# Turning summed tiles back by DMA transposes instead of by TensorE, in a long convolution followed by a quantised feed-forward layer

## The chip, the cores and the metric

One core of a Trainium2 chip runs the whole program. The metric is the time of one execution on the device in microseconds (us), the median of several runs. The engines are TensorE (PE, with its weight loads PEld), VectorE (DVE), ScalarE (ACT), GpSimd (POOL) and SyncE (SP, which here only issues DMAs).

## The reference, cut to what matters

The input `x` is (8, 512, 1024), the context (8, 512, 1024), and there are 64 heads of 8 channels. The first layer (the mixer) takes products of context channels, convolves them over the sequence, and sums them with the normalised input:

```python
kv = einsum('bhil,bhjl->bijhl', k_, v_)              # k = v = context: 8 x 8 products for each head
y = irfft(rfft(kv, 2L) * rfft(ssm_kernel, 2L))[..., :L]   # a causal convolution over L = 1024
out = y + kv * D
out = einsum('bijhl,bhil->bjhl', out, q_)            # q = layernorm(x): summed over i
x = x + tanh(g_xattn) * out                          # the residual
x = x + tanh(g_ffn) * ffn(layernorm(x))              # ffn: layernorm, two linear layers with
                                                     # inputs and weights quantised by blocks of 32
```

The change lies wholly in the way in which `out` gets back to the rows of `x` and is added to them.

## The kernel before, in words

The program has two parts, one after the other: `mixer_block` and `ffn_block`. The change touches the first.

**Heads and tiles.** The mixer goes through 64 heads (`h`), two to a tile (`t = h // 2`, 32 tiles, `TILE_HEADS` = 2). A tile is 128 rows of `x` (2 heads x 8 channels x 8 batches) by 1024 positions. In what follows an even head is the first of its tile, an odd head the second.

**One head.** Positions lie on the partitions while a head is convolved. ACT copies the context tile to PSUM (`copy_k`, L385) and squares it (`squares`, L392); DVE multiplies the other pairs (`make_kk`, L529, L532). ACT rounds the products to their high half (`high_half`, L399), DVE takes the rest (`low_half`, L538). PE multiplies 26 blocks of the convolution three times each, 78 matmuls in five stretches (`conv_stretch`, L328), into a single PSUM tile `y_ps`. DVE multiplies `y_ps` by `q` in two parts (`times_q`, L552, L555, L558) into the two `terms` tiles, and POOL folds each part in four adds (`sum_part`, L763, L765, L767, L769) into `mixed[t % 2]`. PE may start head h + 1 only when `low_half(h + 1)` is done and DVE has read part 0 of head h; a product part may be written only when POOL has folded the one before it in the same `terms` tile.

**Normalising x for q.** For each tile ACT takes the mean and the spread (`ln_stats`, L436, L438, L441), POOL the inverse root (L752), ACT applies both (`ln_apply`, L445, L451). The 32-bit values are then turned by DMA: ACT splits them into low and high 16-bit halves (`split_halves`, L407, into the space of `taps`), SP issues one DMA transpose of both halves (`turn_halves`, L239, into the space of `taps_hi`), and ACT joins them into `q_ext` (`take_q`, L417).

**Turning back.** In an odd head PE transposes the finished tile of the previous pair, `mixed`, by eight matmuls against the identity (`turn_back`, L359) into PSUM (`turn_ps`), after the first stretch of that head. DVE adds `x_tile` to it (`residual`, L681) ahead of `times_q(h, 0)`, and SP stores the sum. PSUM's `turn_ps` is also used four times to spread weight scales (`spread_inverses`, L345), which ACT copies out (`keep_inverses`).

**Other work in the heads.** Each engine's order is written out in a loop over `h`; nothing schedules it but the position in that loop and the semaphores. Weight maxima (L638) come in 32 pieces, up to head 33; then the scales of the weights (L663 to L671) in head 34; then the second layer's weights are quantised in heads 35 to 63 in three steps for each of 16 tiles (`layer2_ints` L647, `layer2_clip` L652, `layer2_quant` L657). Four row tiles are normalised and quantised early, one in every four heads up to head 20 (`early_...`, L580 to L633, L473), and turned by SP's DMA transposes (`turn_early`, L232).

## Time and profile before

| | us |
|---|---|
| median of 3 runs | 1971.43 |
| lowest and highest | 1970.66, 1972.78 |
| the profiled execution, its own time | 1971.53 |
| its span in the trace | 1969.8 |
| PE busy in the span | 1875.5 (95%) |
| DVE busy | 1654.8 (84%) |
| ACT busy | 949.6 (48%) |
| POOL busy | 872.0 (44%) |

The mixer takes roughly the first 1015 us of the span. POOL and ACT have their work mostly there: the shares over the whole span say little of how full they are in it. The position of a head is found in the trace by PE's matmuls: 78 of line L328 are one head, and the first matmul of head 1 starts at 36.68 us, of head 8 at 141.63, of head 21 at 348.54, of head 35 at 560.71, of head 44 at 703.77, of head 63 at 990.11. These five stretches are called stages 1 to 5 below.

### The profile page before, as it was taken

The numbers are of one execution on the slowest core, as the hardware profiler recorded it, in microseconds if no ns is written. First come the engines' busy times: TensorE is split into PE (matmuls) and PEld (weight loads), VectorE is DVE, ScalarE is ACT, GpSimd is POOL, SyncE is SP. The second block draws the span as 40 slices with busy tenths as digits, with TensorE's granted clock in tenths as the row PEclk, the third lists the DMA queues.
The fourth block names the chain that finished last, engine by engine and source line by source line (L and its number), as shares of the span: only waits on it lengthen the run. The fifth ranks groups of instructions, "written<-read, shape, count | busy, mean of one in ns | idle before, by whom it ended". The sixth has DMA issues, their size and how long they took to land. (4 is left out here: it accounts for less than half of the span.)

```text
span 1969.8 us, 28534 instructions
## 1 busy us (share of the span) xinstructions
PE 1875.5 (95%) x11384; PEld 1474.7 (75%) x11432; DVE 1654.8 (84%) x1919; ACT 949.6 (48%) x1227; POOL 872.0 (44%) x645
## 2 busy tenths in 40 slices
PE   6999999999999999999966997999999999999998
PEld 5988888898888888898854665666777766666773
DVE  5889988999888888898789798899888888898843
ACT  5555556555555655555503542444455444444440
POOL 3888788787889889999930000000000000000000
PEclk9999999999999999999978998999999999999999
DMA  6665556677665665767558312221222121221112
GB/s 236 217 208 169 179 163 202 218 274 245 221 209 174 215 208 175 237 189 220 166 202 312 123 39 75 76 75 54 65 76 76 65 68 51 75 76 44 54 43 75
DMA packets 163749, 287.95 MB, mean 146 GB/s; under 512 B 105952, under 2 KB 105952, under 8 KB 155424
## 3 DMA queue, kind: packets, MB, share of 16 engines
q1 hardware_dynamic: 163616, 286.12, 44.2%
q8 instruction: 90, 1.47, 0.3%
q14 instruction: 43, 0.35, 0.1%
HBM read 218.91 MB, written 42.53 MB: 133 GB/s over the span
## 5 line engine op out<-in xcount | busy, mean ns | idle before, releaser
L328 PE MATMUL y_ps<-kk_hi,slab 128*128 128x352 f32 (+6 forms) x3328 | 892.7, 352 | 28.9 <-DMA slab<-taps_scratch 18.1
L328 PEld LDWEIGHTS y_ps<-kk_hi,slab 128*128 128x128 f32 x3328 | 596.7, 190 | 98.1 <-issue 29.8
L328 PE MATMUL y_ps<-kk_lo,slab 128*128 128x512 f32 (+6 forms) x1664 | 582.3, 350 | 0.0
L985 PE MATMUL acc_ps<-w_T,arena 128*128 128x512 bf16 x2000 | 439.5, 379 | 2.5
L970 PE MATMUL l_ps<-f_xq_T,w_T 128*128 128x256 bf16 x3584 | 398.3, 274 | 15.4 <-ACT arena L1031 10.7
L970 PEld LDWEIGHTS l_ps<-f_xq_T,w_T 128*128 128x128 bf16 x3584 | 352.6, 98 | 61.9 <-ACT arena L1031 11.2
L985 PEld LDWEIGHTS acc_ps<-w_T,arena 128*128 128x128 bf16 x2048 | 200.4, 98 | 238.5
L328 PEld LDWEIGHTS y_ps<-kk_lo,slab 128*128 128x128 f32 x1664 | 315.8, 190 | 34.6
L765 POOL TENSOR_TENSOR terms<-terms 128x768 f32<-128x768 f32 x127 | 334.5, 2634 | 10.0
L1031 ACT ACTIVATE arena<-l_ps,f_b 128x256 bf16<-128x256 f32 x512 | 213.4, 474 | 252.3 <-PE l_ps L970 247.4
L1280 POOL TENSOR_TENSOR f_rstd<-f_var_eps,f_neg_half 128x1 f32<-128x1 f32 x28 | 15.4, 549 | 697.7 <-DVE f_var_eps L1090 697.7
L552 DVE TENSOR_TENSOR terms<-y_ps,q_ext 128x768 f32<-128x768 f32 (+1 forms) x128 | 155.9, 1218 | 109.4 <-PE y_ps L328 109.3
L538 DVE TENSOR_TENSOR kk_lo<-kk,kk_hi 128x2304 fp32r<-128x2304 f32 x64 | 183.1, 2861 | 23.6 <-ACT kk_hi L399 23.3
L763 POOL TENSOR_TENSOR terms<-terms 128x72 f32<-128x72 f32 x127 | 144.2, 1135 | 112.6 <-DVE terms L558 112.4
L767 POOL TENSOR_TENSOR terms<-terms 128x384 f32<-128x384 f32 x127 | 181.2, 1427 | 10.0
L417 ACT COPY q_ext<-taps_hi 128x1024 int16<-128x1024 int16 x124 | 105.6, 924 | 107.3 <-DMA taps_hi<-taps 107.3
L399 ACT CAST kk_hi<-kk 128x2304 fp32r<-128x2304 f32 x64 | 136.2, 2128 | 8.2 <-DVE kk L532 6.2
L1010 ACT ACTIVATE f_n<-arena,f_shift,f_rstd 128x1024 bf16<-128x1024 f32 x28 | 34.5, 1239 | 214.2 <-POOL f_shift L1282 214.2
L385 ACT COPY k_ps<-k_ext 128x512 f32<-128x512 f32 x64 | 37.8, 590 | 199.8 <-DVE kk L532 197.0
L1038 ACT ACTIVATE arena<-arena 128x2048 bf16<-128x2048 bf16 x64 | 122.0, 1911 | 0.5
L558 DVE TENSOR_TENSOR terms<-y_ps,q_ext 128x576 f32<-128x576 f32 (+1 forms) x128 | 120.9, 945 | 0.0
L529 DVE TENSOR_TENSOR kk<-k_ps,k_ext 128x1536 f32<-128x1536 f32 x64 | 111.6, 1743 | 0.6 <-ACT k_ps L385 0.6
(130 smaller groups left out, 1880.8 us busy)
## 6 DMA issues: line engine op xcount, KB each, us to landing
slab<-taps_scratch SPq DMA_DIRECT2D x128, 512.0 KB, 4.9
arena<-in_w_m SPq DMA_DIRECT2D x32, 1024.0 KB, 6.2
arena<-x_scratch SPq DMA_DIRECT2D x60, 512.0 KB, 3.8
k_ext<-in_ctx_e SPq DMA_DIRECT2D x64, 384.0 KB, 3.4
arena<-in_w SPq DMA_DIRECT2D x18, 1024.0 KB, 6.5
x_tile<-in_x_t SPq DMA_DIRECT2D x32, 512.0 KB, 4.9
out_t<-arena SPq DMA_DIRECT2D x32, 512.0 KB, 2.6
x_scratch<-x SPq DMA_DIRECT2D x31, 512.0 KB, 3.3
```

The lines of the kernel that those rows point to most:

```text
L328: mm = nc.tensor.matmul(y_ps[:, y_base + begin:y_base + end], slab[s][:, half, d * P:(d + 1) * P], kk_part[s][:, begin - d * PAIR:end - d ...
L399: nc.scalar.copy(kk_hi[h % 2][:], kk[:].rearrange("p n c -> p (n c)")).then_inc(hi_ready, 1)
L538: nc.vector.tensor_tensor(kk_lo[h % 2][:], kk[:].rearrange("p n c -> p (n c)"), kk_hi[h % 2][:].bitcast(F32), ALU.subtract).then_inc(lo_re ...
L552: nc.vector.tensor_tensor(view(term, 0, [(pitch, count), (CH, DIAG), (1, CH)]), view(y_ps, y_at, [(PAIR, count), (CH, DIAG), (1, CH)]), vi ...
L558: nc.vector.tensor_tensor(view(term, UPPER_ROWS * CH + B, [(pitch, count), (CH + B, 3), (1, CH)]), view(y_ps, y_at + CH, [(PAIR, count), ( ...
L763: add(term[:, :, 0:FOLD], term[:, :, 0:FOLD], term[:, :, 8 * CH:8 * CH + FOLD], ALU.add).then_inc(wrapped, 1)
L765: add(term[:, :, 0:4 * CH], term[:, :, 0:4 * CH], term[:, :, 4 * CH:8 * CH], ALU.add).then_inc(four_rows, 1)
L767: add(term[:, :, 0:2 * CH], term[:, :, 0:2 * CH], term[:, :, 2 * CH:4 * CH], ALU.add).then_inc(two_rows, 1)
L970: mm = nc.tensor.matmul(l1_ps[bank % L1_BANKS][:, a, :], w1_T[:, b, k, a * P:(a + 1) * P], inputs[:, k, :], start=(k == 0), stop=(k == L / ...
L985: mm = nc.tensor.matmul(acc_ps[s][:, c * 512:(c + 1) * 512], hidden[g % 2][:, k, s * P:(s + 1) * P], w2_T[:, k, c * 512:(c + 1) * 512], st ...
L1031: done = nc.scalar.activation(hidden[g % 2][:, c, :], l1_ps[bank % L1_BANKS][:, a, :], ACT.Identity, bias=b1_c[:, c:c + 1])
L1038: nc.scalar.activation(h, h, ACT.Gelu_apprx_tanh).then_inc(gelu_ready, 1)
```

## The change

The tiles 0 to 30 are no longer turned back by PE. In an odd head ACT splits the summed tile of the previous pair into 16-bit halves (`split_mixed`) and issues a DMA transpose of them itself; in the next even head it joins the turned halves into the 32-bit tile `x1` (`merge_back`), and DVE adds `x_tile` to it in place (`residual`), now at the end of the even head's order, after `low_half`. Only the last tile still goes through PE (`turn_last`, `last_residual`). The space of the halves is shared with the turning of q, so each user waits for the other. The transposes for q and the early tiles are also issued by ACT now, not by SP. ACT's order in a head is recast: squares first, then in even heads the statistics of the next tile, then the high half, then the copy of the context. Early steps, weight maxima and what follows them start one head later; the second layer's weights are spread over 28 heads instead of 29.

```diff
-    maxima_heads = list(range(6)) + list(range(7, early_heads + 5, 2))
+    maxima_heads = list(range(6)) + list(range(8, early_heads + 6, 2))
...
-                if h % TILE_HEADS == 1 and t + 1 < tiles:
-                    turn_halves(t + 1)
-                if h % TILE_HEADS == 1 and t >= 1:
-                    store_x1(t - 1)
-                    if t + 3 < tiles:
-                        load_x(t + 3)
-                if h >= 9 and h % 4 == 1 and (h - 9) // 4 < EARLY:
-                    turn_early((h - 9) // 4)
+                if h % TILE_HEADS == 0 and t >= 2:
+                    store_x1(t - 2)
+                    if t + 2 < tiles:
+                        load_x(t + 2)
...
-                pe.wait_ge(x1_ready, spread_heads[r] // TILE_HEADS - 1)
+                if r == 0:
+                    pe.wait_ge(q_ready, 1)
+                else:
+                    pe.wait_ge(inv_kept, r)
                 for n in range(LB):
                     mm = nc.tensor.matmul(turn_ps[:, n, :], inv_rows[:, n * P:(n + 1) * P], ident_bf[:], start=True, stop=True)
                 mm.then_inc(inv_spread, 1)
 
-            def turn_back(t):
-                pe.wait_ge(sums_ready, min(2 * TILE_HEADS * (t + 1), 2 * heads - 1))
-                if t == tiles - 1:
-                    pe.wait_ge(last_sums, 1)
-                if TILE_HEADS * (t + 1) in spread_heads:
-                    pe.wait_ge(inv_kept, spread_heads.index(TILE_HEADS * (t + 1)) + 1)
-                if t == 0:
-                    pe.wait_ge(q_ready, 1)
-                else:
-                    pe.wait_ge(x1_ready, t)
+            def turn_last():
+                t = tiles - 1
+                pe.wait_ge(sums_ready, 2 * heads - 1)
+                pe.wait_ge(last_sums, 1)
+                pe.wait_ge(inv_kept, len(spread_heads))
...
-                    if h % TILE_HEADS == 1 and i == 0 and t >= 1:
-                        turn_back(t - 1)
-            turn_back(tiles - 1)
+            turn_last()
...
+                if t >= 3:
+                    act.wait_ge(mixed_turned, 16 * (t - 2))
                 nc.scalar.copy(xn_halves, xn[:].bitcast(I16).rearrange("p (l h) -> p h l", h=2)).then_inc(halves_ready, 1)
+                act.wait_ge(halves_ready, t)
+                if t >= 3:
+                    act.wait_ge(back_merged, t - 2)
+                act.dma_start(q_halves, xn_halves.rearrange("p h l -> p (h l)"), transpose=True).then_inc(halves_turned, 16)
+
+            def turn_early(u):
+                act.wait_ge(x_quant, u + 1)
+                act.dma_start(first_inputs(arena, u // GROUP)[:, :, u % GROUP * P:(u % GROUP + 1) * P], n_bf[u % 2],
+                              transpose=True).then_inc(e_turned[u % 2], 16)
+
+            def split_mixed(t):
+                act.wait_ge(sums_ready, 2 * TILE_HEADS * (t + 1))
+                act.wait_ge(halves_turned, 16 * min(t + 2, tiles - 1))
+                nc.scalar.copy(xn_halves, mixed[t % 2][:].rearrange("p n c -> p (n c)").bitcast(I16)
+                               .rearrange("p (l h) -> p h l", h=2)).then_inc(mixed_split, 1)
+                act.wait_ge(mixed_split, t + 1)
+                act.wait_ge(q_ready, min(t + 3, tiles))
+                act.dma_start(q_halves, xn_halves.rearrange("p h l -> p (h l)"), transpose=True).then_inc(mixed_turned, 16)
+
+            def merge_back(t):
+                act.wait_ge(mixed_turned, 16 * (t + 1))
+                if t >= 2:
+                    act.wait_ge(x1_stored[t % 2], 16 * (t // 2))
+                if t % 2 == 0 and 1 <= t // 2 <= EARLY:
+                    act.wait_ge(e_norm, t // 2)
+                words = view(x1[t % 2].bitcast(I16), 0, [(2, L // QB), (2 * L // QB, QB), (1, 2)])
+                source = view(taps_hi_all.bitcast(I16), 0, [(QB, L // QB), (1, QB), (LB * P, 2)])
+                nc.scalar.copy(words, source).then_inc(back_merged, 1)
...
-            ln_stats(1)
             for h in range(heads):
                 t = h // TILE_HEADS
+                if h + 1 < heads:
+                    squares(h + 1)
+                if h % TILE_HEADS == 0 and t + 1 < tiles:
+                    ln_stats(t + 1)
+                if h + 1 < heads:
+                    high_half(h + 1)
                 if h + 2 < heads:
                     copy_k(h + 2)
-                if h + 1 < heads:
-                    squares(h + 1)
-                    high_half(h + 1)
                 if t + 1 < tiles:
                     if h % TILE_HEADS == 0:
+                        if t >= 2:
+                            merge_back(t - 2)
                         ln_apply(t + 1)
                         split_halves(t + 1)
                     else:
                         take_q(t + 1)
-                        if t + 2 < tiles:
-                            ln_stats(t + 2)
-                if h >= 4 and h % 4 == 0 and h // 4 - 1 < EARLY:
+                        if t >= 1:
+                            split_mixed(t - 1)
+                elif h % TILE_HEADS == 0:
+                    merge_back(t - 2)
+                else:
+                    split_mixed(t - 1)
+                if h >= 5 and h % 4 == 1 and h // 4 - 1 < EARLY:
                     early_norm(h // 4 - 1)
+                if h >= 10 and h % 4 == 2 and (h - 10) // 4 < EARLY:
+                    turn_early((h - 10) // 4)
                 if h + 1 in spread_heads:
                     repeat_inverses(spread_heads.index(h + 1))
                 if h in spread_heads:
                     keep_inverses(spread_heads.index(h))
+            merge_back(tiles - 2)
...
-                dve.wait_ge(back_ready, t + 1)
-                if 2 <= t < tiles - 1:
-                    dve.wait_ge(x1_stored[t % 2], 16 * (t // 2))
-                if t % 2 == 0 and 1 <= t // 2 <= EARLY:
-                    dve.wait_ge(e_norm, t // 2)
-                out = x1_last if t == tiles - 1 else x1[t % 2][:]
-                nc.vector.tensor_tensor(out.rearrange("p (i k) -> p i k", i=QB),
+                dve.wait_ge(back_merged, t + 1)
+                nc.vector.tensor_tensor(x1[t % 2][:], x1[t % 2][:], x_tile[:, t % X_SLOTS, :], ALU.add).then_inc(x1_ready, 1)
+
+            def last_residual():
+                t = tiles - 1
+                dve.wait_ge(back_ready, 1)
...
-                if h % TILE_HEADS == 1 and t >= 1:
-                    residual(t - 1)
                 times_q(h, 0)
                 if h + 1 < heads:
                     low_half(h + 1)
-                if h >= 3 and h % 4 == 3 and h // 4 < EARLY:
-                    early_statistics(h // 4)
+                if h % TILE_HEADS == 0 and t >= 2:
+                    residual(t - 2)
+                if h >= 4 and h % 4 == 0 and h // 4 - 1 < EARLY:
+                    early_statistics(h // 4 - 1)
...
             times_q(heads - 1, 1)
+            residual(tiles - 2)
             last_part()
             first_ints(dve)
-            residual(tiles - 1)
+            last_residual()
...
+                if t >= 2 and part == 0:
+                    pool.wait_ge(mixed_split, t - 1)
```

ACT in an even head (head 22) before, from the copy of the context for two heads ahead to the split of the normalised tile (`k_ps` and `kk` are the context and its products, `xn` the normalised tile, `taps` the space of its halves):

```order
L385 COPY k_ps<-k_ext 128x512 [waits kk_ready,k_loaded0]
L392 ACTIVATE kk<-k_ext 128x8x64 [waits hi_ready,lo_ready,k_loaded1]
L399 CAST kk_hi<-kk 128x2304 [waits y_ready,kk_ready,squares_ready]
L445 ACTIVATE shift<-neg_mean,rstd 128x1 [waits rstd_ready]
L451 ACTIVATE xn<-x_tile,shift,rstd 128x1024 [waits halves_ready,shift_ready]
L407 COPY taps<-xn 128x2048 [waits halves_turned,xn_ready]
```

Head 22 of the changed kernel:

```order
L375 ACTIVATE kk<-k_ext 128x8x64 [waits hi_ready,lo_ready,k_loaded1]
L449 ACTIVATE xn,neg_mean<-x_tile 128x1024 [waits halves_ready,x_loaded0]
L451 ACTIVATE xn,spread_sum<-x_tile,neg_mean 128x1024 [waits mean_ready]
L454 ACTIVATE var_eps<-spread_sum 128x1 [waits spread_ready]
L382 CAST kk_hi<-kk 128x2304 [waits y_ready,kk_ready,squares_ready]
L368 COPY k_ps<-k_ext 128x512 [waits kk_ready,k_loaded0]
L420 COPY x_1<-taps_hi 128x32x32x2 [waits x1_stored1,mixed_turned]
L458 ACTIVATE shift<-neg_mean,rstd 128x1 [waits rstd_ready]
L464 ACTIVATE xn<-x_tile,shift,rstd 128x1024 [waits halves_ready,shift_ready]
L392 COPY taps<-xn 128x2048 [waits mixed_turned,halves_turned,xn_ready]
L396 DMA_TRANSPOSE taps_hi<-taps 128x16x128 [waits back_merged,halves_ready]
```

The statistics came in from the odd head and stand ahead of the high half, the join (L420) and the transpose (L396) are new on ACT.

ACT in the odd head of the same pair (head 23) before, after its high half:

```order
L417 COPY q_ext<-taps_hi 128x8x128 [waits products_ready,halves_turned]
L417 COPY q_ext<-taps_hi 128x8x64
L417 COPY q_ext<-taps_hi 128x8x128
L417 COPY q_ext<-taps_hi 128x8x64
L436 ACTIVATE xn,neg_mean<-x_tile 128x1024 [waits halves_ready,x_loaded1]
L438 ACTIVATE xn,spread_sum<-x_tile,neg_mean 128x1024 [waits mean_ready]
L441 ACTIVATE var_eps<-spread_sum 128x1 [waits spread_ready]
```

And in the changed kernel, from the squares to the second transpose:

```order
L375 ACTIVATE kk<-k_ext 128x8x64 [waits hi_ready,lo_ready,k_loaded0]
L382 CAST kk_hi<-kk 128x2304 [waits y_ready,kk_ready,squares_ready]
L368 COPY k_ps<-k_ext 128x512 [waits kk_ready,k_loaded1]
L430 COPY q_ext<-taps_hi 128x8x128 [waits products_ready,halves_turned]
L430 COPY q_ext<-taps_hi 128x8x64
L430 COPY q_ext<-taps_hi 128x8x128
L430 COPY q_ext<-taps_hi 128x8x64
L406 COPY taps<-mixed 128x2048 [waits halves_turned,sums_ready]
L410 DMA_TRANSPOSE taps_hi<-taps 128x16x128 [waits q_ready,mixed_split]
```

The statistics have left the odd head; the split of the summed tile (L406) and its transpose (L410) have come in, and the squares of the next even head stand behind them.

DVE in an odd head before, from the products to the low half (`x_0` is the tile `x1[0]`):

```order
L529 TENSOR_TENSOR kk<-k_ps,k_ext 128x8x192 [waits k_copied,lo_ready]
L532 TENSOR_TENSOR kk<-k_ps,k_ext 128x8x32
L681 TENSOR_TENSOR x_0<-turn_ps,x_tile 128x1024 [waits x1_stored0,back_ready]
L552 TENSOR_TENSOR terms<-y_ps,q_ext 128x3x256 [waits sums_ready,y_ready]
L555 TENSOR_TENSOR terms<-y_ps,q_ext 128x3x64
L558 TENSOR_TENSOR terms<-y_ps,q_ext 128x3x3x64
L538 TENSOR_TENSOR kk_lo<-kk,kk_hi 128x2304 [waits hi_ready,squares_ready]
```

DVE in an even head of the changed kernel, from the second products to the first of the next head:

```order
L556 TENSOR_TENSOR kk<-k_ps,k_ext 128x8x32
L576 TENSOR_TENSOR terms<-y_ps,q_ext 128x3x256 [waits sums_ready,q_ready,y_ready]
L579 TENSOR_TENSOR terms<-y_ps,q_ext 128x3x64
L582 TENSOR_TENSOR terms<-y_ps,q_ext 128x3x3x64
L562 TENSOR_TENSOR kk_lo<-kk,kk_hi 128x2304 [waits hi_ready,squares_ready]
L700 TENSOR_TENSOR x_1<-x_1,x_tile 128x1024 [waits back_merged]
```

The residual (now L700) left its place between the products and `times_q`, stands behind the low half, and reads two SBUF tiles instead of one in PSUM and one in SBUF.

## Rows read from the trace of the kernel before

**Rows 1.** The page's busy times: time, share of the span, instructions.

```profile
PE 1875.5 (95%) x11384; PEld 1474.7 (75%) x11432; DVE 1654.8 (84%) x1919; ACT 949.6 (48%) x1227; POOL 872.0 (44%) x645
```

**Rows 2.** Busy time by engine: stages 1 to 5 (length, PE, PEld, DVE, ACT, POOL; clock, DMA).

```profile
36.68:141.63 104.95, 104.95 (x572) 93.76 (x573) 90.61 (x90) 58.04 (x62) 87.04 (x62) 1.00 0.64 205
141.63:348.54 206.91, 200.34 (x1065) 178.79 (x1063) 186.58 (x187) 116.91 (x124) 167.78 (x121) 0.98 0.57 182
348.54:560.71 212.17, 211.04 (x1155) 188.48 (x1154) 188.99 (x161) 119.40 (x127) 171.86 (x120) 1.00 0.70 242
560.71:703.77 143.06, 138.46 (x777) 123.16 (x775) 123.03 (x105) 83.19 (x89) 125.66 (x77) 1.00 0.61 191
703.77:990.11 286.34, 285.12 (x1557) 254.49 (x1556) 247.51 (x212) 154.71 (x162) 262.12 (x162) 1.00 0.62 194
```

**Rows 3.** The same view of line L328 alone: an odd head, then an even one.

```profile
440.31:455.74 15.43, 14.80 (x79) 12.99 (x79) 1.00 0.70 215
455.74:470.31 14.57, 14.57 (x81) 12.97 (x80) 1.00 0.75 297
```

**Rows 4.** PE in order of time around a turning back (start, length, instruction).

```profile
443.29 0.30 PE L328 MATMUL y_ps<-kk_hi,slab 128*128 128x288 f32 x1
443.43 1.04 PE L359 MATMUL turn_ps<-ident,mixed 128*128 128x128 f32 x8
444.22 0.47 PE L328 MATMUL y_ps<-kk_hi,slab 128*128 128x512 f32 x1
```

**Rows 5.** DVE in order of time: the starts of heads 8 and 12 on DVE.

```profile
143.68 1.48 DVE L552 TENSOR_TENSOR terms<-y_ps,q_ext 128x1280 f32<-128x1280 f32 x1
...
207.83 1.48 DVE L552 TENSOR_TENSOR terms<-y_ps,q_ext 128x1280 f32<-128x1280 f32 x1
```

**Rows 6.** Waits in stage 2: total us, times, longest.

```profile
DVE terms L552 <- PE y_ps L328: 14.1, 10, 2.8
...
PE y_ps L328 <- issue: 6.5, 3, 2.2
DVE kk_lo L538 <- ACT kk_hi L399: 4.0, 9, 0.6
```

**Rows 7.** Groups of ACT with shapes apart: count, busy us and mean ns, idle before.

```profile
L399 ACT CAST kk_hi<-kk 128x2304 fp32r<-128x2304 f32 x64 | 136.2, 2128 | 8.2 <-DVE kk L532 6.2
...
L451 ACT ACTIVATE xn<-x_tile,shift,rstd 128x1024 f32<-128x1024 f32 x32 | 75.0, 2343 | 1.1
L417 ACT COPY q_ext<-taps_hi 128x1024 int16<-128x1024 int16 x62 | 72.7, 1173 | 107.3 <-DMA taps_hi<-taps 107.3
...
L407 ACT COPY taps<-xn 128x2048 int16<-128x2048 int16 x31 | 58.9, 1901 | 1.0
```

**Rows 8.** The DMA transposes of q on SP's queue: issue in ns, landing in us.

```profile
L239 SPq DMA_TRANSPOSE taps_hi<-taps x31: 2713/3167/3892, 45.3 to 962.2; - x31
...
DMA to landing us min/median/max: 4.2/5.0/6.3
```

**Rows 9.** POOL in order of time beside DVE's old residual and low half.

```profile
165.68 2.98 POOL L765 TENSOR_TENSOR terms<-terms 128x1280 f32<-128x1280 f32 x1
...
171.24 2.65 POOL L763 TENSOR_TENSOR terms<-terms 128x72 f32<-128x72 f32 x1
173.97 1.84 POOL L765 TENSOR_TENSOR terms<-terms 128x768 f32<-128x768 f32 x1
```

**Rows 10.** DVE in order of time in the same stretch.

```profile
166.99 1.21 DVE L681 TENSOR_TENSOR x<-turn_ps,x_tile 128x1024 f32<-128x1024 f32 x1
...
170.58 3.12 DVE L538 TENSOR_TENSOR kk_lo<-kk,kk_hi 128x2304 fp32r<-128x2304 f32 x1 [0.58 <-ACT kk_hi L399]
```

**Rows 11.** Single lines: shortest, median and longest ns.

```profile
L538 DVE TENSOR_TENSOR kk_lo<-kk,kk_hi x64: 2546/2998/3676, 13.5 to 984.5; 128x2304 fp32r<-128x2304 f32 x64
...
L763 POOL TENSOR_TENSOR terms<-terms x127: 333/453/2663, 31.9 to 1000.7; 128x72 f32<-128x72 f32 x64, 128x120 f32<-128x120 f32 x63
...
L652 DVE TENSOR_SCALAR arena<-arena x16: 678/832/2231, 578.0 to 989.5; 128x2048 int16<-128x2048 int16 x16
```

**Rows 12.** Waits in stage 5.

```profile
POOL terms L763 <- DVE terms L558: 15.1, 15, 1.4
...
PE y_ps L328 <- issue: 1.2, 2, 0.9
```

**Rows 13.** The end of the mixer on PE.

```profile
1010.76 1.94 PE L359 MATMUL turn_ps<-ident,mixed 128*128 128x128 f32 x8 [6.39 <-issue]
```

More of the change, by code:

```diff
@@ L86, in mixer_block @@
     early_heads = 4 * EARLY
-    maxima_heads = list(range(6)) + list(range(7, early_heads + 5, 2))
-    maxima_heads += [early_heads + 5 + 2 * n // 3 for n in range(2 * W_TILES - len(maxima_heads))]
+    maxima_heads = list(range(6)) + list(range(8, early_heads + 6, 2))
+    maxima_heads += [early_heads + 6 + 2 * n // 3 for n in range(2 * W_TILES - len(maxima_heads))]
     maxima_of = [[n for n in range(2 * W_TILES) if maxima_heads[n] == h] for h in range(heads)]
@@ L306, in _ @@
                 sp.wait_ge(turned, 16 * EARLY // 2)
+            store_x1(tiles - 2)
             for parity in range(2):
@@ L698, in _ @@
                     low_half(h + 1)
-                if h >= 3 and h % 4 == 3 and h // 4 < EARLY:
-                    early_statistics(h // 4)
-                if h >= 5 and h % 4 == 1 and h // 4 - 1 < EARLY:
+                if h % TILE_HEADS == 0 and t >= 2:
+                    residual(t - 2)
+                if h >= 4 and h % 4 == 0 and h // 4 - 1 < EARLY:
+                    early_statistics(h // 4 - 1)
+                if h >= 6 and h % 4 == 2 and h // 4 - 1 < EARLY:
                     early_second_statistics(h // 4 - 1)
-                if h >= 6 and h % 4 == 2 and h // 4 - 1 < EARLY:
+                if h >= 7 and h % 4 == 3 and h // 4 - 1 < EARLY:
                     early_input(h // 4 - 1)
-                if h >= 8 and h % 4 == 0 and h // 4 - 2 < EARLY:
+                if h >= 9 and h % 4 == 1 and h // 4 - 2 < EARLY:
                     early_quantise(h // 4 - 2)
@@ L776, in _ @@
                     inv_sqrt(h // TILE_HEADS + 1)
-                if h >= 4 and h % 4 == 0 and h // 4 - 1 < EARLY:
+                if h >= 5 and h % 4 == 1 and h // 4 - 1 < EARLY:
                     early_rstd(h // 4 - 1)
-                if h >= 6 and h % 4 == 2 and h // 4 - 1 < EARLY:
+                if h >= 7 and h % 4 == 3 and h // 4 - 1 < EARLY:
                     early_second_rstd(h // 4 - 1)
```

11 lines of the change are left out of this document (2 added, 9 removed).

## The prediction

> **What bounds the kernel now.** I read the page's busy times first: PE has 95% of the span [rows 1]. Then the busy time by stage of the mixer, which the change alone touches: in stages 1, 3 and 5 PE is busy for all but 0 to 1.2 us; in stage 2 it stands still for 6.6 of 206.91 us and in stage 4 for 4.6 of 143.06 [rows 2]. So mostly the mixer goes at the speed of PE. But the same rows show DVE busy for 86 to 90% of each stage, and POOL for 92% of stage 5 (262.12 of 286.34): what PE gives up can soon meet another engine. Third, PE's convolution alone: an odd head lasts 15.43 us, an even head 14.57, with the same 78 matmuls [rows 3]. Fourth, PE in order of time: the eight transposes start at 443.43 and the next convolution matmul at 444.22, against 0.14 from one matmul to the next ahead of them [rows 4]. So the turning back costs PE 15.43 - 14.57 = 0.86 us in each odd head.
>
> **1. PE.** 31 of 32 turnings go: 3, 6, 7, 5 and 9 in the five stages and one in head 63. The 30 in the stages give 0.86 x 30 = 25.8 us if PE stays the bound. The spread of scales still uses `turn_ps`, but its waits fall on other spreads, not on the heads.
>
> **2. DVE.** The old residual reads PSUM and one SBUF tile: 1.21 us [rows 10]. The new one is 1024 elements from two SBUF tiles. No row shows it; L538 does 2304 such elements in 2546 ns at its shortest [rows 11], 1.1 ns each, so 1.1 us, between that and 1.4 with contention. Its own length is no gain and no loss. What differs is POOL. While the old residual ran (166.99 to 168.20), POOL's fold L765 (165.68, 2.98 us) was not held up; when L538, with two SBUF inputs, ran from 170.58 to 173.70, POOL's L763 took 2.65 us in place of 0.33, and ended just after it [rows 9 to 11]. L538 itself is 3.12 instead of 2.55 there. L652 is 678 ns at best and 2231 at worst [rows 11]. So instructions of DVE with two SBUF inputs and POOL's folds exclude each other one by one. I take the new residual to be of that kind: it takes 1.1 us from POOL in each pair of heads, and waits some 0.4 us for POOL itself. At the least it takes nothing, at the most it also waits for a whole L765 (2.98 us).
>
> The Trainium skill (SBUF — State Buffer, Who interferes with whom) has this as a rule: a VectorE instruction with two SBUF inputs contends with a GpSimd instruction that reads SBUF, one with at most one does not, and the loser waits for the whole instruction. The rows on L681 and L538 agree with it; without the rule's step from L538 to the new residual, stage 5 below would come out some 11 us lower.
>
> **3. ACT.** It had 119.40 us of work in stage 3, seven pairs of heads: 17.1 us for a pair [rows 2]. New for a pair:
> - the split of the summed tile: as L407, 1.90 us [rows 7];
> - the join: 2048 16-bit elements, read alternately from two places 2048 bytes apart, written two at a time every 128 bytes. L417 reads in the same alternate way at 1173/1024 = 1.1 ns an element, L407 goes at 0.93, L451, which reads 4 bytes every 128 bytes, at 2343/1024 = 2.3 [rows 7]. So between 1.9 and 4.7 us; I take 2.1, near L417 and L407, because two of its writes lie side by side;
> - two transposes issued by ACT. On SP's queue each held the queue for 3.17 us, 2.7 to 3.9 [rows 8]. No row shows one on ACT; I take the same, 6.3 us for the pair (5.4 to 7.8).
>
> Sum: 17.1 + 1.9 + 2.1 + 6.3 = 27.4 us, against 29.14 for PE without turnings (2 x 14.57). It fits, with 1.7 us to spare, but what ACT does late is now the high half: in the odd head split, transpose, squares and statistics all stand ahead of the next one. Against that, squares and the copy no longer stand between the products and the high half; DVE's waits for the high half were 4.0 us in stage 2 [rows 6], and they go as long as ACT is on time.
>
> By the Trainium skill (SBUF — State Buffer, Door 1: The DMA port swizzle) each access that crosses into another 16-byte line pays a penalty. L451 fits that and L417 does not: it crosses at every read and is twice as fast per element. By the rule the join would take 4.7 us and the pair 30.0; by L417's row it does not.
>
> **4. SP and DMA.** SP loses 3.17 us of issue in odd heads, and it was not waited for. A second transpose of the same size in each pair adds load to DMA engines that are 57 to 70% busy [rows 2]; landing took 4.2 to 6.3 us [rows 8], and there is about a head between issue and use. Nothing for this. The stores of `x1` now wait on DVE at the end of an even head, with the next slab loads behind them; they have a head's 14.57 us of room.
>
> **5. By stage, against 1971.53, the profiled execution.**
> - Stage 1, heads 1 to 7: 3 x 0.86 = -2.6.
> - Stage 2, heads 8 to 20. Four heads last 207.83 - 143.68 = 64.15 us [rows 5], where PE alone would need 60.0. DVE is the bound with hand-overs to ACT. Per four heads (3.25 of them) DVE waits 14.1 / 3.25 = 4.3 us for PE, of which 1.7 go with two turnings; 4.0 / 3.25 = 1.2 for the high half go; the residual's waits for POOL add 0.8. That gives 62.0, -2.1 per four heads, -6.8 in all, and PE's three stalls of 2.2 us [rows 6] are part of that. In these heads ACT has early work besides (L473 and a third transpose every four heads), so it will be late at times: I take -4, with 0 and -6.8 as ends.
> - Stage 3, heads 21 to 34: 7 x 0.86 = -6.0; DVE at 188.99 of 206.2 and POOL at 171.86 still have room; I take -5.5.
> - Stage 4, heads 35 to 43: at most 5 x 0.86 = -4.3 and PE's 4.6 us idle, -8.9; POOL is at 125.66 of 143.06 with weights being quantised. I take -5.
> - Stage 5, heads 44 to 62: PE gives 9 x 0.86 = -7.7. POOL waited for DVE's products for only 15.1 us of 286.34 [rows 12]. Asked of that room: 7.7 by the shorter heads, 10 residuals x 1.15 = 11.5, and 1.6 because 16 weight tiles now lie in 28 heads instead of 29 (DVE's three steps, some 4.5 us for a tile, 0.085 us a head). Together 20.8, or 5.7 more than there is. With no waiting left at all the stage would be 7.7 - 5.7 = 2 us shorter; with all of POOL's old waits kept, 20.8 - 7.7 = 13 longer. Full packing is what PE now has and POOL never had; I take +1.5, nearer to the first, because POOL's waits shrink when it is what others wait for.
> - End: the residual of tile 30 now stands before the last folds, on the chain to PE's last transposes, which waited 6.39 us at 1010.76 [rows 13]: +1.1.
>
> Sum: -2.6 - 4 - 5.5 - 5 + 1.5 + 1.1 = -14.5, so 1957.0. The median of the runs is 0.1 us from the profiled execution, so 1957 stands for both.
>
> **Rivals.**
> - *All fits.* POOL gives way, PE is the bound in every stage: -2.6 - 6.8 - 6.0 - 8.9 - 7.7 + 1.1 = -30.9, 1941. For it: PE has been idle for only 1.2 us in stage 5 [rows 12]. Against it: POOL's 92% there.
> - *POOL takes it all back.* Stage 2 gives 2, stage 3 gives 4, and stage 5 keeps all of POOL's waits: -2.6 - 2 - 4 - 5 + 13 + 1.1 = +0.5, 1972. That is no change.
> - *ACT becomes the bound, slower than before.* Its place is the odd head: split, transpose, squares, statistics, then the high half. The old mixer needed (990.11 - 36.68) / 31 = 30.76 us for a pair; ACT's pair is 27.4 by my values. It decides from 3.4 us more, and each further us costs 31. The join at 4.7 (+2.6), the transposes at 3.9 each (+1.5) and a wait for POOL's inverse root in the even head (some 0.9) make 32.4; some of these together, at 31.5, give 0.74 x 31 + 1.1 = +24, 1996. For it: two of three prices are shown by no row. Against it: L407 and L417.
> - *The change does not do what it says* has no room here: the transposes are gone from PE by its order.
>
> **Chances.** The forecast (1948 to 1967) 0.45, all fits 0.18, POOL takes it back 0.16, ACT the bound 0.21. A measurement of this kernel tells about 0.2% (4 us) from no change. Faster 0.62, within 0.2% 0.16, slower 0.22. The range is 1938 to 1990: below lies little of the second case, above about half of the last.
>
> **What would show it.** Right: even and odd heads both near 14.6 in stages 1 and 3; the new residual at 1.1 to 1.5 us with POOL's fold beside it stretched; the join near 2.1 and the two transposes near 3.2 us on ACT's queue; POOL's waits for the products in stage 5 well under 15 us and heads there near 15.1; waits of DVE for the high half rare. Wrong: DVE waiting for the high half in most even heads (then ACT is the bound), a join over 3 us, PE without a stall in stage 5 (then POOL was no limit), or slab loads that PE waits for.

## The result: slower by 3%

| | before | changed |
|---|---|---|
| median of 4 runs each, us | 1971.05 | 2029.68 |
| lowest to highest | 1970.63 to 1972.78 | 2020.84 to 2040.35 |
| profiled execution, its span | 1971.53, 1969.8 | 2020.84, 2018.9 |

The ratio is 1.030, with a 95% interval of 1.0273 to 1.0327. The forecast was 1957.0 with a range up to 1990, so the time lies outside it. The profiled execution is the fastest of the four; where I divide up time by traces, I use the difference of the traces, 49 us, not that of the medians, 59.

### The profile page after: what moved, and what is told of

Same layout as the page of the kernel before. It is cut to its first block and busy times, and to the rows that moved or that the text cites. A ratio compares the mean times of both kernels' runs of the same rounds, so it can differ in the third digit from the quotient of the medians.

```text
span 2018.9 us, 28209 instructions
## 1 busy us (share of the span) xinstructions
PE 1873.1 (93%) x11184; PEld 1462.5 (72%) x11184; DVE 1682.2 (83%) x1919; ACT 1062.3 (53%) x1289; POOL 883.7 (44%) x645
## 5 line engine op out<-in xcount | busy, mean ns | idle before, releaser
L315 PE MATMUL y_ps<-kk_hi,slab 128*128 128x352 f32 (+6 forms) x3328 | 900.9, 354 | 87.4 <-issue 62.0
L315 PEld LDWEIGHTS y_ps<-kk_hi,slab 128*128 128x128 f32 x3328 | 604.8, 192 | 161.7 <-issue 83.7
L315 PE MATMUL y_ps<-kk_lo,slab 128*128 128x512 f32 (+6 forms) x1664 | 586.3, 352 | 0.0
L1012 PE MATMUL acc_ps<-w_T,arena 128*128 128x512 bf16 x2048 | 444.5, 379 | 0.0
L315 PEld LDWEIGHTS y_ps<-kk_lo,slab 128*128 128x128 f32 x1664 | 319.3, 192 | 34.6
L562 DVE TENSOR_TENSOR kk_lo<-kk,kk_hi 128x2304 fp32r<-128x2304 f32 x64 | 196.9, 3077 | 81.0 <-ACT kk_hi L382 80.9
L794 POOL TENSOR_TENSOR terms<-terms 128x384 f32<-128x384 f32 x127 | 201.1, 1584 | 10.0
L796 POOL TENSOR_TENSOR mixed<-terms 128x192 f32<-128x192 f32 x127 | 169.8, 1337 | 10.0
L382 ACT CAST kk_hi<-kk 128x2304 fp32r<-128x2304 f32 x64 | 135.9, 2123 | 40.6 <-DVE kk L556 39.8
L790 POOL TENSOR_TENSOR terms<-terms 128x72 f32<-128x72 f32 x127 | 83.6, 659 | 147.4 <-DVE terms L582 147.4
L375 ACT ACTIVATE kk<-k_ext 128x512 f32<-128x512 f32 x64 | 40.5, 632 | 196.2 <-issue 196.2
L430 ACT COPY q_ext<-taps_hi 128x1024 int16<-128x1024 int16 x124 | 105.1, 920 | 16.5 <-DMA taps_hi<-taps 16.5
```

Source lines behind the costliest of these rows:

```text
L315: mm = nc.tensor.matmul(y_ps[:, y_base + begin:y_base + end], slab[s][:, half, d * P:(d + 1) * P], kk_part[s][:, begin - d * PAIR:end - d ...
L382: nc.scalar.copy(kk_hi[h % 2][:], kk[:].rearrange("p n c -> p (n c)")).then_inc(hi_ready, 1)
L562: nc.vector.tensor_tensor(kk_lo[h % 2][:], kk[:].rearrange("p n c -> p (n c)"), kk_hi[h % 2][:].bitcast(F32), ALU.subtract).then_inc(lo_re ...
L794: add(term[:, :, 0:2 * CH], term[:, :, 0:2 * CH], term[:, :, 2 * CH:4 * CH], ALU.add).then_inc(two_rows, 1)
L796: add(out, term[:, :, 0:CH], term[:, :, CH:2 * CH], ALU.add).then_inc(sums_ready, 1)
L1012: mm = nc.tensor.matmul(acc_ps[s][:, c * 512:(c + 1) * 512], hidden[g % 2][:, k, s * P:(s + 1) * P], w2_T[:, k, c * 512:(c + 1) * 512], st ...
```

## The profile after

First the page's busy times (after's lines: convolution L315, squares L375, high half L382, `take_q` L430, join L420, low half L562, residual L700, folds L790 to L796).

```profile
PE 1873.1 (93%) x11184; PEld 1462.5 (72%) x11184; DVE 1682.2 (83%) x1919; ACT 1062.3 (53%) x1289; POOL 883.7 (44%) x645
```

PE has the turnings less but is not less busy: 1873.1 against 1875.5 [rows 1]. Next the same five stages as in [rows 2], with the same columns, and the sum that the view gives.

```profile
35.24:140.16 104.92, 102.34 (x547) 90.71 (x546) 83.05 (x81) 63.84 (x64) 86.17 (x64) 1.00 0.75 207
140.16:351.65 211.49, 192.55 (x1015) 169.52 (x1015) 195.76 (x193) 140.36 (x137) 172.56 (x118) 1.00 0.64 185
351.65:576.76 225.11, 209.34 (x1094) 185.46 (x1093) 196.80 (x161) 144.34 (x141) 176.55 (x121) 0.98 0.78 241
576.76:724.57 147.81, 136.16 (x726) 120.59 (x725) 123.33 (x103) 95.69 (x92) 125.35 (x80) 0.98 0.70 208
724.57:1034.05 309.48, 288.71 (x1489) 257.06 (x1487) 260.33 (x215) 197.82 (x190) 261.26 (x158) 0.96 0.71 201
sum 998.81, PE 929.09 PEld 823.34 DVE 859.27 ACT 642.06 POOL 821.89; mean PE 185.82 PEld 164.67 DVE 171.85 ACT 128.41 POOL 164.38
```

The stages are 45.4 us longer than before (998.81 against 953.43, the sum of [rows 2]); the other 3.7 us of the 49 lie outside them. The starts of heads are found by counting matmuls, of which a few records are missing. Found by the change of shape that begins a head instead, they lie up to 2.3 us off, and all five stages together are 47.9 us longer; single stages are no more exact than that. PE is idle for 69.7 us in them, DVE for 140, POOL for 177: no engine is full. Which wait ends last says who is late. The waits from 40 to 1040 us (total us, times, longest):

```profile
ACT kk L375 <- issue: 194.6, 49, 7.3
POOL terms L790 <- DVE terms L582: 143.2, 51, 7.0
DVE kk_lo L562 <- ACT kk_hi L382: 77.3, 45, 5.0
...
PE y_ps L315 <- issue: 62.0, 36, 4.3
DVE terms L576 <- PE y_ps L315: 59.0, 37, 3.6
ACT shift L458 <- POOL rstd L777: 53.8, 22, 3.9
```

The same window of the kernel before has, for the third of these lines:

```profile
DVE kk_lo L538 <- ACT kk_hi L399: 19.1, 26, 1.7
```

DVE waits for the high half 77.3 us instead of 19.1, and ACT stands still ahead of the squares for 194.6 us that the view calls issue. What it did there is on the lines of its two transposes (count, shortest, median and longest ns of the issue):

```profile
L396 ACTq DMA_TRANSPOSE taps_hi<-taps x31: 1332/4921/7482, 36.3 to 1005.7; - x31
L410 ACTq DMA_TRANSPOSE taps_hi<-taps x31: 1332/1864/6307, 79.9 to 1036.2; - x31
```

On SP's queue before, all lay between 2.7 and 3.9 us [rows 8]. Here one takes 1.33 us at its shortest and 7.48 at its longest; the means are 4.70 (L396) and 2.63 (L410). What precedes a long one is seen on SP's queue and ACT (start, length), around the transpose of q in head 26:

```profile
449.39 0.32 SPq L236 DMA_DIRECT2D x_scratch<-x  x1
449.75 1.36 SPq L200 DMA_DIRECT2D x_tile<-in_x_t  x1
451.15 0.45 SPq L217 DMA_DIRECT2D arena<-in_w_m  x1
451.65 0.90 SPq L208 DMA_DIRECT2D slab<-taps_scratch  x2
460.48 0.33 SPq L203 DMA_DIRECT2D k_ext<-in_ctx_e  x1
```

```profile
451.36 1.90 ACT L392 COPY taps<-xn 128x2048 int16<-128x2048 int16 x1
453.29 6.35 ACTq L396 DMA_TRANSPOSE taps_hi<-taps  x1
459.77 0.63 ACT L375 ACTIVATE kk<-k_ext 128x512 f32<-128x512 f32 x1 [6.51 <-issue]
```

As soon as the residual is done, SP issues a store, a load of x, weights and slabs (449.39 to 452.55); the transpose behind them holds ACT for 6.35 us. SP itself issues nothing while it lasts: its last issue ended 0.74 us before, its next one starts at 460.48. Last the chain of one stall of PE, at the start of head 29. It begins half a head later, with the transpose of the summed tile:

```profile
468.19 3.78 ACTq L410 DMA_TRANSPOSE taps_hi<-taps  x1
...
472.09 0.63 ACT L375 ACTIVATE kk<-k_ext 128x512 f32<-128x512 f32 x1 [3.93 <-issue]
...
475.18 2.11 ACT L382 CAST kk_hi<-kk 128x2304 fp32r<-128x2304 f32 x1
...
477.39 4.23 DVE L562 TENSOR_TENSOR kk_lo<-kk,kk_hi 128x2304 fp32r<-128x2304 f32 x1 [1.64 <-ACT kk_hi L382]
...
479.28 3.21 POOL L794 TENSOR_TENSOR terms<-terms 128x384 f32<-128x384 f32 x1
...
481.54 2.02 DVE L700 TENSOR_TENSOR x<-x,x_tile 128x1024 f32<-128x1024 f32 x1
481.72 0.40 PE L315 MATMUL y_ps<-kk_hi,slab 128*128 128x352 f32 x1 [1.65 <-issue]
```

The products were ready at 472.28, the squares only at 472.72, behind the transpose; statistics and high half follow, so the low half starts at 477.39 and PE at 481.72. The low half takes 4.23 us instead of 2.55 with POOL's fold beside it, and that fold (L794, 3.21 us instead of 1.03 in the head before) is stretched too. This is the rarer of two places. Sorted by head, 30 of DVE's 47 waits for the high half in the whole mixer (57.5 of 80.9 us) are for an even head, behind the transpose of q, and 17 (23.4 us) for an odd head, behind that of the summed tile. PE's stalls at the start of a head (from 0.3 us up) come to 47.7 us in 27 even heads and 14.9 us in 9 odd ones.

Then the clock. A stretch with a stall of 4.04 us ahead of even head 60, and the next 78 matmuls (length, PE, PEld; granted clock, DMA; by count, so the first begins in the last microsecond of head 59):

```profile
983.61:1004.91 21.30, 17.26 (x77) 15.58 (x77) 0.84 0.48 136
1004.91:1019.48 14.57, 14.57 (x81) 12.97 (x80) 1.00 0.83 253
```

After idle time PE gets the lower of its two levels (1.2 instead of 2.4 GHz) for part of the stretch, a mean of 0.84, and the same matmuls take 17.26 us instead of 14.57.

## The experiments

Each is told with the time of its runs' median; the kernel before had 1969.8 to 1970.7 in the batches. "On SP" is short for the first one.

**All transposes on SP's queue.** ACT still splits and joins.

```diff
-                act.dma_start(q_halves, ..., transpose=True).then_inc(halves_turned, 16)
-                act.dma_start(q_halves, ..., transpose=True).then_inc(mixed_turned, 16)
...
+                if h % TILE_HEADS == 1 and t + 1 < tiles:      # SP, right behind load_slab(h + 1)
+                    turn_halves(t + 1)
+                if h % TILE_HEADS == 0 and t >= 2:
+                    turn_mixed(t - 2)
```

> The changed kernel with all three kinds of DMA transposes issued by SP again, in each head right behind the slab loads; ACT still splits and joins. If ACT's queue being held by the transposes is the cause (4.70 us mean for the one of q, 2.63 for the summed tile, 7.3 us a pair of heads), the high half comes in time, waits of DVE for it fall from 77 us to under 20, and the time falls from 2030 to between 1945 and 1975. If the SBUF residual's clash with POOL, or the split and the join themselves, are the cause, it stays above 2005.

Measured: 1960.0 (1956.8 to 1961.9), ratio 0.9943 (0.9929 to 0.9958), in the first range, and the waits of DVE for the high half are under the 20 us expected:

```profile
DVE kk_lo L573 <- ACT kk_hi L407: 16.7, 34, 1.6
```

The 70 us by which the changed kernel is above it hang on who issues, and the rest of the change is a gain of 0.6%. Its stages:

```profile
35.69:137.89 102.20, 102.20 (x549) 90.98 (x549) 85.62 (x83) 64.72 (x66) 87.09 (x63) 1.00 0.76 213
137.89:344.22 206.33, 191.75 (x1008) 168.57 (x1006) 195.61 (x190) 137.89 (x136) 170.85 (x118) 1.00 0.69 190
344.22:556.14 211.92, 205.96 (x1094) 182.41 (x1093) 197.84 (x162) 144.54 (x141) 177.78 (x122) 1.00 0.83 256
556.14:691.20 135.06, 133.29 (x728) 118.42 (x727) 126.89 (x104) 96.97 (x94) 127.13 (x77) 1.00 0.78 229
691.20:974.94 283.74, 280.37 (x1494) 249.18 (x1492) 261.08 (x215) 197.72 (x190) 273.31 (x163) 0.99 0.76 218
sum 939.25, PE 913.57 PEld 809.56 DVE 867.03 ACT 641.84 POOL 836.16; mean PE 182.71 PEld 161.91 DVE 173.41 ACT 128.37 POOL 167.23
```

ACT is as busy as in the changed kernel (641.8 and 642.1): its computing isn't the matter. Of 59.6 us between the sums, 15.5 are PE at work (929.09 - 913.57, the clock) and 44.0 PE idle (69.7 - 25.7).

**One operand of the residual in PSUM**, in the changed kernel. Outside four tiles the sum leaves out the mixer's result.

```diff
-                nc.vector.tensor_tensor(x1[t % 2][:], x1[t % 2][:], x_tile[:, t % X_SLOTS, :], ALU.add)
...
+                other = x1[t % 2][:] if first <= t <= last else turn_ps[:].rearrange("p n c -> p (n c)")
+                nc.vector.tensor_tensor(x1[t % 2][:], other, x_tile[:, t % X_SLOTS, :], ALU.add)
```

> The changed kernel, but DVE's residual reads PSUM and x_tile in place of two SBUF tiles, outside heads 38 to 44; it leaves out the mixer's result in these tiles. If the clash with POOL is the cause, the residual takes 1.2 us instead of 1.9, and most of the 58 us come back: under 1995. If ACT's lateness is the cause, POOL and DVE gain 0.7 us a pair that nobody waits for: 2015 to 2035.

Measured: 2002.4 (2000.6 to 2011.3), between the two expectations: 27 us. So the clash counts, but ACT's lateness is the larger part. The same edit on SP:

> The kernel with all transposes on SP (1960.0), with the residual reading PSUM and the tile of x instead of two SBUF tiles, outside tiles 17 to 20; the mixer's result is left out of the sum there. Theory B, the residual with two SBUF inputs and POOL's folds exclude each other and this costs time: 1.1 to 1.5 us for each of 31 pairs of heads where POOL or DVE is near its limit, so 8 to 25 us: 1935 to 1952. Rival A (once ACT is on time the clash is covered): 1956 to 1962. In the changed kernel the same edit gave 27 us (2029.7 to 2002.4), but there it also shortened DVE's part of a chain that ACT had made late.

Measured: 1949.1 (1948.3 to 1949.8), 10.9 us less, in the range of the clash. The residual's line there, and in the changed kernel:

```profile
L715 DVE TENSOR_TENSOR x<-turn_ps,x_tile x27: 1209/1211/1224, 92.4 to 983.4; 128x1024 f32<-128x1024 f32 x27
```

```profile
L700 DVE TENSOR_TENSOR x<-x,x_tile x31: 1210/1886/2851, 94.5 to 1052.8; 128x1024 f32<-128x1024 f32 x31
```

Never over 1.22 us with an operand in PSUM, mostly 1.89 with two in SBUF. The rule of the Trainium skill (SBUF — State Buffer, Who interferes with whom) is borne out in this form: beside POOL's folds the addition is stretched with two inputs in SBUF and not with one.

**The kernel before with its transposes issued by ACT**, nothing else changed.

> The kernel before, with one thing of the change alone: the transposes of q and of the early tiles are issued by ACT, not by SP. ACT then has 17.1 + about 4.7 us of work in a pair of heads of 30.8, so by the theory that ACT is overfilled it still fits: 1968 to 1985. If a transpose issued from ACT hurts in itself (it delays slab loads or holds the high half back at once), over 1990.

Measured: 1982.4 (1981.0 to 1984.2), ratio 1.0062 (1.0045 to 1.0079): 11 to 12 us, in the first range. Alone, without split, join and second transpose, it costs little. Its transposes took 1.33/1.90/5.42 us (shortest, median, longest); SP's store and load were issued in the odd head there, the transposes in the even one.

**The kernel before with squares and high half ahead of the copy.**

> The kernel before, with ACT's squares and high half ahead of the copy of the context, and nothing else of the change. DVE waited 23 us in all for the high half, which this takes 0.5 us forward; where PE is the bound nothing changes, in stage 2 (heads 8 to 20) DVE is. Expected 3 to 8 us faster than before, 1963 to 1968. If the recast order is itself harmful, slower than 1975.

Measured: 1965.1 (1963.9 to 1966.7), ratio 0.9972 (0.9961 to 0.9982), as expected: about half as much as all on SP gains.

**Only the summed tiles' transposes on ACT.**

> The changed kernel, with the transposes of q and of the early tiles issued by SP again, behind its slab loads; ACT issues only the transposes of the summed tiles, in odd heads. In the changed kernel ACT's queue was held 4.70 us by each transpose of q (31 of them) and 2.63 us by each of a summed tile. Theory A, what costs is the time that ACT's queue is held and the length of that hold: the larger part of the 70 us between the changed kernel (2029.7) and the one with all transposes on SP (1960.0) goes: 1965 to 1985. Rival A2, what costs is the transpose in the odd head, which stands ahead of the squares of the next even head: little goes, 2005 to 2025. Rival D, what counts is any traffic on ACT's own DMA queue beside SP's: in between, 1985 to 2005.

Measured: 2000.8 (2000.5 to 2003.3). 29 of the 70 us go, 41 are left by 31 holds in odd heads, 2.86 us at the median. The larger part was expected to go by the theory that the time held is what costs, and didn't. The time lies in the range of the third expectation, traffic on ACT's own queue; the unread copies below decide between the two.

**Statistics behind high half and copy**, in the changed kernel and on SP.

```diff
-                if h % TILE_HEADS == 0 and t + 1 < tiles:
-                    ln_stats(t + 1)
                 if h + 1 < heads:
                     high_half(h + 1)
                 if h + 2 < heads:
                     copy_k(h + 2)
+                if h % TILE_HEADS == 0 and t + 1 < tiles:
+                    ln_stats(t + 1)
```

> The changed kernel, with the statistics of the next tile (3.7 us, in even heads) behind the high half and the copy of the context, no longer ahead of the high half. Theory A (the issue of transposes holds ACT): the transposes still stand ahead of the next squares, but 3.7 us of work leaves the way to the high half in every second head, so some of the loss goes: 1995 to 2020. Rival C, the new place of the statistics is the main cost: under 1985. Rival E, the statistics run in time that ACT spent waiting anyway, and POOL's inverse root comes later now: no gain or a loss, 2025 to 2045.

> The kernel with all transposes on SP (1960.0), with the statistics behind the high half and the copy. Rival C (the place of the statistics costs something of its own): under 1955. Theory A (ACT is on time once its queue is free, so the order in it no longer matters): 1956 to 1965. Rival E (the inverse root on POOL comes late, ACT waits for it longer than the 82.6 us it waits now): 1965 to 1985.

Measured: 2046.3 (2043.7 to 2046.8), 17 us more, and on SP 2000.8 (2000.2 to 2003.5), 41 us more. My theory expected a gain and no change; both times lie above every range written down, the first just, the second by 16 us. A wait on SP shows part of it:

```profile
ACT kk_hi L407 <- issue: 281.7, 59, 8.7
```

It was 86.1 before that edit. The high half has to wait in any case; with the statistics ahead of it they fill this wait, with the statistics behind it all that ACT does after them comes later. DVE now waits 32.3 us for the join (0.3 before the edit) and PE 28.3 us for DVE's products (6.1). ACT waits for POOL's inverse root for only 4.9 us instead of 82.6, so the sign that the rival gave, a longer wait there, did not show. Their new place in the change is a good one.

**Holds of ACT without a transpose.** On SP, with 512-element copies (0.65 us from one to the next) that nothing reads, behind each split: seven and four, two and two, as many in each tile as the changed kernel's holds (147 and 82 us in all), and those of one kind alone. The odd ones alone follow the kernel with only the summed tiles on ACT (90 us).

```diff
                 nc.scalar.copy(xn_halves, xn[:]...).then_inc(halves_ready, 1)
+                for _ in range(7):      # behind split_mixed: 4
+                    pad()
```

> The kernel with all transposes on SP (1960.0), plus copies on ACT that nothing reads, 512 elements each (the squares, as long, take 0.63 us): seven right behind the split of the normalised tile and four right behind the split of the summed tile, so that ACT is held about 4.6 and 2.6 us where the changed kernel held it 4.70 and 2.63 us for the issue of a transpose. Theory A, the whole loss lies in the time that ACT is held there: 2015 to 2040. Rival F, the loss is rather that the transposes go through a second DMA queue beside SP's, and late transposes and slabs: under 1990. Between the two, the hold's share of the 70 us is (result - 1960) / 70.

> The same with two copies at each place, about 1.3 us each: what the issue of a transpose costs ACT at its shortest (1.33 us). Theory A: ACT has this room, so 1960 to 1972. Rival G, ACT's order has no room at all in an even head and each us held there counts at once, 31 x 2.6 = 81 us: over 1985.

> As the kernel with seven and four unread copies (1996.4), but with as many copies (0.65 us each) in each tile as the changed kernel's trace shows for that transpose: 2 to 12 behind the split of the normalised tile (146.9 us in all), 2 to 10 behind that of the summed tile (81.9 us). The sum is that of the changed kernel and within 8 us of seven and four (221 us). Theory A with uneven holds (what counts is how far a single hold goes beyond the room that ACT has there, so long ones cost more than short ones give back): 2010 to 2035. Rival F (the rest of the loss isn't ACT's time, but what the transposes on a second DMA queue do to transfers and landings): 1988 to 2003.

> The kernel with all transposes on SP (1960.0), with unread copies behind the split of the summed tile alone, in odd heads, as many in each tile as the holds that the trace of the kernel with only the summed tiles' transposes on ACT shows (2 to 9 copies, 90.4 us in all). That kernel took 2000.8. If its loss of 41 us is ACT's time in odd heads: 1990 to 2005. If the even and the odd head have the same room, this should be in proportion to the 229 us of both (44 us for 229): 1975 to 1980. If the second DMA queue does most of the harm by itself: 1965 to 1975.

> The same with the copies behind the split of the normalised tile alone, in even heads, 2 to 12 in each tile, 146.9 us in all, as the changed kernel's trace has them. If a hold in an even head has more room, since in the odd head that follows the high half comes right behind the squares: 1962 to 1980. If the long holds of even heads do most of what both did together (2004.4): 1985 to 2000.

| copies behind the splits (even, odd heads) | us | lowest to highest | above 1960.0 |
|---|---|---|---|
| 2, 2 | 1965.4 | 1962.4 to 1968.5 | 5 |
| 7, 4 | 1996.4 | 1995.1 to 1997.8 | 36 |
| 2 to 12, 2 to 10, as in the changed kernel | 2004.4 | 2003.0 to 2006.4 | 44 |
| none, 2 to 9, as with only summed tiles on ACT | 1997.7 | 1996.7 to 1999.6 | 38 |
| 2 to 12, none | 1997.4 | 1993.7 to 1999.7 | 37 |

Against what was expected: two and two as the theory had it; seven and four between the two theories; the full replay just above the range by which the rest is not ACT's time (up to 2003), below the other (from 2010); the odd ones alone in the first range, the even ones alone in the second. So ACT's time is most of the loss, not all of it. Alone, with every transpose on SP, it makes 44 of the 70 us by the medians; by the traces, with the profiled execution at 2018.9 against 2003.8, 49 of 64. Short holds fit nearly; holds less than three times as long (7.2 us a pair instead of 2.6) cost seven times as much. Holds in odd heads cost 38 us for 90 us held, in even heads 37 for 147, and both together (82 us odd, 147 even) little more than either. And 38 of the 41 us of the kernel with only the summed tiles on ACT are ACT's time.

**SP's store and load of x in the odd head**, in the changed kernel and on SP.

```diff
-                if h % TILE_HEADS == 0 and t >= 2:
+                if h % TILE_HEADS == 1 and t >= 2:
                     store_x1(t - 2)
```

> The changed kernel, with the store of the summed tile and the load of the next tile of x, which SP issues in an even head as soon as the residual is done, moved to the odd head behind it; all transposes stay on ACT. Theory H, the transposes of q are issued slowly because SP's transfers of the even head are ahead of them: their median falls from 4.92 us to under 3, those of the summed tiles in odd heads rise by about 1 us, and the time falls to 1995 to 2015. Rival: the weights and slabs of the even head do it alone, or SP no longer waits for the residual ahead of the slab loads but that didn't matter: 2020 to 2035.

> The same move of SP's store and load to the odd head, on the kernel with all transposes on SP (1960.0). There ACT is not held, so theory A says 1955 to 1962; if SP's wait for the residual ahead of the next slab loads costs PE something (PE waits 19.0 us for what the trace doesn't name), 1945 to 1955; if the store and load now delay the transpose of q or the slabs in the odd head, 1962 to 1975.

Measured: 1996.4 (1989.4 to 2010.8), in the first range, 33 us less, though every transpose is still on ACT; on SP 1960.0 (1958.4 to 1963.1), no change, as expected for an ACT that isn't held. The two transposes of the first:

```profile
L396 ACTq DMA_TRANSPOSE taps_hi<-taps x31: 1333/1928/4129, 36.3 to 989.5; - x31
...
L410 ACTq DMA_TRANSPOSE taps_hi<-taps x31: 1333/3887/7750, 80.0 to 1017.7; - x31
```

The medians have changed places (1.93 and 3.89, after 4.92 and 1.86): the hold goes to whichever transpose is issued behind SP's batch. It isn't a swap alone. All holds together are 174 us instead of 227 (5.6 us a pair instead of 7.3), so part of the 33 us is shorter holding; how much of it wasn't separated.

Why an issue grows stays open. The profile counts an issue from the end of its semaphore waits and includes the wait for a descriptor generator that two issuing engines share and that is free again before an issue ends, says the Trainium skill (Perfetto Trace Analysis, DMA Instruction — HWDGE). That wait does not explain the long ones. On SP, where ACT issues nothing, moving the store and load swaps the two transposes as well, from 5.11 and 3.09 at the median to these:

```profile
L242 SPq DMA_TRANSPOSE taps_hi<-taps x31: 1322/1937/4999, 36.7 to 955.9; - x31
L247 SPq DMA_TRANSPOSE taps_hi<-taps x31: 2836/5202/9347, 80.1 to 980.8; - x31
```

And of the 26 transposes of q over 3 us in the changed kernel, 17 began when SP's last issue had ended, as the one of 6.35 us above. So a transpose behind that batch is long whoever issues it; on ACT it holds computing. The DMA engines were full during that one (share 1.00), but also during one of 1.33 us at 437.86 (0.98), so their load alone doesn't set it either. That issuing on several engines saves sequencer time that is usually small next to the transfer, says the Trainium skill (DMA: Bandwidth & Descriptors, Issuing engines are not separate DMA queues); this does not hold here, where the median issue of q took ACT 4.92 us and the median from issue to landing was 8.3 us.

## Why the prediction was wrong, step by step

1. **PE, 25.8 us: right in size.** Heads without a stall last 14.57 us, odd ones too (1004.91 to 1019.48 above). On SP the stages are 14.2 us shorter than before by the traces (forecast for the change: 15.6): -2.7, -0.6, -0.3, -8.0 and -2.6, where the forecast had -2.6, -4, -5.5, -5 and +1.5. That the sums lie close is partly luck, since stages 2 and 3 gave less and stages 4 and 5 more (with the starts found by shape, the 14.2 are 12.2).
2. **The residual: its wait too low.** 1.89 us at the median, 0.7 above its shortest 1.21, instead of 1.1 plus a wait of 0.4; the mutual exclusion was right, and costs 11 us even where ACT is on time, 27 where it isn't.
3. **ACT: the failed step is "It fits, with 1.7 us to spare", from which no loss was put into any stage but the second.** Its terms were near: ACT's own work 642.06 / 31 = 20.7 us a pair (forecast 17.1 + 1.9 + 2.1 = 21.1), the join among it 2.17 (forecast 2.1, as L417's row had it, not the 4.7 of L451's), the two transposes 7.3 instead of 6.3. The sum is 28.0, still under PE's 29.14. But fitting in the sum isn't being on time. ACT also waits: 53.8 us for POOL's inverse root and 39.8 for DVE's products, 3.0 us a pair, which with the rest makes 31.0 of the 32.2 that a pair lasts (998.81 / 31). It cannot make up a hold of up to 7.5 us in the few us ahead of the next high half. I took 3.17 us, a steady figure of SP's queue [rows 8], as the price on another engine's queue; it was 3.7 on average but 1.3 to 7.5 singly, longest behind what SP had just issued, and the change itself had put SP's batch ahead of it. With the holds replayed on SP this step is worth 49 of the 64 us by the traces.
4. **"Nothing for this" on SP and DMA: wrong by that batch.** Moving it alone gives 33 us, all of it through ACT's holds as far as is known, since on SP the same move changes nothing. Slabs were not late: PE waited for one once in the stages, 0.8 us.
5. **The end: +1.1, measured +1.5** (PE waits 7.94 us for its last turning, 6.39 before [rows 13]). The turning that head 63 no longer holds gives 0.86 of it back, which the sum left out.

The rival "ACT becomes the bound" named the engine and the direction, and the sign of a wrong forecast, DVE waiting for the high half, is what the trace shows. Its place was half right: it looked at the split, the transpose and the statistics ahead of the high half of an odd head, which DVE does wait for in 17 of 32 even heads, but more than twice as much is lost behind the transpose of q, which the same sum had at 3.17 us. Its criterion, 3.4 us more ACT work in a pair, was wrong (0.6 more was enough), as was its price (24 us for the change, 49 by the trace): ACT's work never became the bound in the sum, and the stall of PE took the clock along, 15.5 us that no step had. It also blamed the statistics, which do no harm there.

**Open.** 15 us by the traces (25 by the medians) between the changed kernel and the replay of its holds on SP. It may be that real holds fall together with SP's batches and the replayed ones don't; I did not test it. The replay also leaves out the holds of the four early transposes (1.33 to 2.67 us each), and what makes an issue long is not shown. The changed kernel and the one with SP's store moved also scatter by 20 us over four runs, all others by 1 to 11 us, which I can't explain.

The best kernels that compute everything are the two with all transposes on SP, 1960.0, 0.6% faster than before.

## What to carry to other kernels

A DMA issued by a computing engine is an instruction of that engine, and its length can depend on what another queue issued just before (1.33 to 7.75 us here); look at the longest, not the mean, and ask what stands behind it and how soon it is needed. An engine whose work fits in the sum can still be late in each round: look at its waits beside its work, and compare a single hold with the room ahead of the next hand-over. A wait that looks idle may be the best place for other work, and whoever moves that work out of it pays.

## What the runs showed of the hardware that I had not expected

- The issue of the same DMA transpose (128 x 16 x 128, 16-bit) takes ACT 1.33 us at its shortest, less than SP ever needed before (2.71), and up to 7.75. SP gets down to 1.32 too, once its store and load stand elsewhere, so this isn't a matter of the engine; and long ones also occur when SP issues nothing meanwhile.
- PE's granted clock was 0.84 over a stretch of 21.30 us with 4.0 us of idle time, and 1.00 in the next, which had none.
- The join, which crosses from one 2048-byte half to the other at every element, ran at 1.06 ns an element (2170 / 2048).
